# Order of the cross-attention steps: rows turned ahead of the shifted scores, tail rows both in bank 0, first maxima in slot 7

## What is computed

```python
x = x + attn_window(_layernorm(x))              # L0: 16 heads of 16, |i-j| <= 32
x = x + xattn_pad(ctx, ctx, _layernorm(x))      # keys padded per item
x = x + top2_of_8_experts(_layernorm(x))        # softmax gate, two gelu layers
x = x + attn_causal(_layernorm(x))              # L1
x = x + xattn_mask(_layernorm(x), ctx, ctx)     # one mask for all rows
x = x + quantised_ffn(_layernorm(x))            # scale is a maximum over all rows
```

## Time and profile before

| | |
|---|---|
| median of 3 runs | 2198.09 us (2197.56 to 2198.1) |
| the profiled execution: its own time, its span | 2189.82 us, 2188.2 us |
| PE busy, share of the span | 1992.9 us, 91% |
| DVE, ACT, POOL busy | 1245.5, 965.0, 688.6 us (57%, 44%, 31%) |
| granted PE clock in the mean | 0.974 |

### The profile page before, as it was taken

One profiled execution on the slowest core, in us unless ns is written; L12 is line 12 of the kernel. 1 busy time (PEld: TensorE's weight loads), 2 busy tenths in 40 slices (PEclk: granted clock), 3 DMA queues, 4 the chain that ended last, 5 costly groups with the idle time before them and its releaser, 6 DMA issues. The chain is left out here.

```text
span 2188.2 us, 51471 instructions
## 1 busy us (share of the span) xinstructions
PE 1992.9 (91%) x17362; PEld 1531.9 (70%) x17362; DVE 1245.5 (57%) x5443; ACT 965.0 (44%) x1849; POOL 688.6 (31%) x1254
## 2 busy tenths in 40 slices
PE   7999998999967999999999799999988887999869
PEld 5777776666646999999998577777666664444357
DVE  5778885566641101111115688888777775459964
ACT  3455555666632333333333255555545553357400
POOL 3566665245561000000001545553422220013400
PEclk9999999999978999999999899999999998999989
DMA  7333332233319999999995644333233321000023
GB/s 216 108 106 108 103 122 86 89 106 111 112 68 359 376 339 346 337 347 336 347 335 190 186 127 135 122 125 108 83 99 97 95 92 43 0 0 1 0 58 96
DMA packets 209108, 334.50 MB, mean 153 GB/s; under 512 B 59453, under 2 KB 193250, under 8 KB 199874
## 3 DMA queue, kind: packets, MB, share of 16 engines
q1 hardware_dynamic: 194482, 301.82, 39.6%
q0 software_dynamic: 9552, 26.10, 3.9%
q10 hardware_dynamic: 4928, 4.72, 0.6%
HBM read 193.74 MB, written 28.05 MB: 101 GB/s over the span
## 5 line engine op out<-in xcount | busy, mean ns | idle before, releaser
L1913 ACT ACTIVATE moe_h<-moe_h_ps,moe_weights 128x128 f32<-128x128 f32 x424 | 132.8, 364 | 254.3 <-PE moe_h_ps L1885 226.0
L2344 PE MATMUL ffn_prod_ps<-x_sb,ffn_weights 128*128 128x512 f32 x480 | 210.9, 599 | 9.7 <-ACT ffn_sig_q L2330 7.0
L1251 ACT ACTIVATE causal_prob<-causal_ps 128x768 f32<-128x768 f32 (+1 forms) x192 | 168.7, 879 | 113.2 <-PE causal_ps L1500 111.8
L1945 DVE TENSOR_TENSOR moe_y<-moe_y_ps,moe_weights 128x256 f32<-128x256 f32 x53 | 22.5, 425 | 328.1 <-PE moe_y_ps L1895 328.1
L1885 PE MATMUL moe_h_ps<-moe_h,moe_weights 128*128 128x128 f32 x1696 | 198.0, 275 | 0.0
L1832 POOL DMA_DIRECT2D moe_y_dram<-moe_y x71 | 39.4, 555 | 494.6 <-DVE moe_y L1945 494.6
L1885 PEld LDWEIGHTS moe_h_ps<-moe_h,moe_weights 128*128 128x128 f32 x1696 | 193.6, 192 | 0.1
L2344 PEld LDWEIGHTS ffn_prod_ps<-x_sb,ffn_weights 128*128 128x128 f32 x480 | 91.0, 192 | 127.2 <-issue 110.2
L984 DVE CUSTOM_DVE_ANT_0 causal_masked<-causal_ps,causal_causal_mask 128x256 bf16<-128x256 f32 (+1 forms) x512 | 152.4, 354 | 45.2 <-PE causal_ps L1466 43.5
L984 DVE CUSTOM_DVE_ANT_0 window_masked<-window_ps,window_window_mask 128x160 bf16<-128x160 f32 x512 | 135.3, 320 | 60.4 <-PE window_ps L1466 57.8
L1251 ACT ACTIVATE window_prob<-window_ps 128x640 f32<-128x640 f32 x128 | 90.0, 703 | 97.7 <-PE window_ps L1500 96.2
(11 more groups left out here) (376 smaller groups left out, 4675.8 us busy)
## 6 DMA issues: line engine op xcount, KB each, us to landing
moe_weights<-moe_w_in SPq DMA_DIRECT2D x53, 2180.0 KB, 9.0
q_pair<-parts SPq DMA_DIRECT2D x512, 128.0 KB
parts<-moe_w_in SPq DMA_DIRECT2D x18, 2180.0 KB, 8.9
k_pair<-parts SPq DMA_DIRECT2D x256, 128.0 KB
k_pair<-parts SPq DMA_DIRECT2D x256, 38.5 KB
moe_rows<-moe_slots_dram SPq DMA_DIRECT2D x71, 128.0 KB, 3.1
moe_y_dram<-moe_y POOLq DMA_DIRECT2D x71, 128.0 KB, 3.4
x_before_ffn_dram<-x_sb SPq DMA_DIRECT2D x16, 256.0 KB, 2.2
```

The source lines that it names most:

```text
L1251: nc.scalar.activation(out, src, ACT.Exp).then_inc(expd, 1)
L1913: nc.scalar.activation(out[:, f, :], psum[:, f // 2, (f % 2) * TM:(f % 2) * TM + TM], ACT.Gelu, bias=bias[:, f:f + 1]).then_inc(done, 1)
L2344: op = nc.tensor.matmul(prod_ps[:, slot, f, :].rearrange("p (b t) -> p b t", b=2), w[:, k, at:at + P], x_cols(n // GROUPS, k), start=(k == ...
```

## The change

Four edits, on PE, ACT and DVE; on POOL and SP no instruction moves. For steps with shifted scores of a cross item (refs 18 to 33, new helper `wide`):

1. PE turns the rows of the new item (L1598) ahead of the shifted scores of slot 0, not behind them.
2. The first half's maxima (`max_out` hf 0 and `max_rows`) go from slots 4 and 5 to slot 7: on PE ahead of the output projection, on ACT behind the exponentials of slot 6.

In tail steps:

3. Both tail halves use columns 256 on of bank 0. The second now waits for the first's evacuation (`last_ev`), and no longer for `q_lo` and `added`; ACT evacuates it in slot 4 behind the exponentials and ahead of v, where it was behind v.
4. DVE makes the low parts of q ahead of the tail's statistics in slot 2.

```diff
+        def wide(ref):
+            return active(ref, 2) and layer_at(ref, 2).pairs == 2
...
+                        if i == 2 and active(ref, 0):
+                            low_part(q_parts[par], q_ps, layer_at(ref).bq, q_hi, q_lo, t, S)
                         if i == 2 and in_tail(ref, 4):
...
-                        if i == 2 and active(ref, 0):
-                            low_part(q_parts[par], q_ps, layer_at(ref).bq, q_hi, q_lo, t, S)
...
                     act.wait_ge(last_mm, e * 2 + k + 1)
-                    if k == 1 and active(ref, 0):
-                        act.wait_ge(v_ev, t + 1)
...
-                    nc.scalar.activation(out, bank(k)[:, S:2 * S], ACT.Copy).then_inc(last_ev, 1)
+                    nc.scalar.activation(out, bank(0)[:, S:2 * S], ACT.Copy).then_inc(last_ev, 1)
...
-                        if i == 5 and in_tail(ref, 5):
-                            keep_turned(t, ref, 1)
-                        if i == 5 and active(ref, 1):
+                        if i == 5 and active(ref, 1) and not wide(ref):
                             max_rows(t, 1, 0)
...
+                        if i == 4 and in_tail(ref, 5):
+                            keep_turned(t, ref, 1)
+                        if i == 7 and active(ref, 1) and wide(ref):
+                            max_rows(t, 1, 0)
...
-                        op = nc.tensor.transpose(bank(k)[:, S + s * P:S + s * P + P],
+                        op = nc.tensor.transpose(bank(0)[:, S + s * P:S + s * P + P],
...
                         if active(ref, 1):
                             scores(t, ref, i)
+                        if i == 0 and active(ref, 0) and wide(ref):
+                            turn_normed(t, ref)
...
                         if i == 4 and in_tail(ref, 5):
-                            wait(pe, q_lo, upto(t, ref, 0))
-                            wait(pe, added, upto(t, ref, 4))
+                            pe.wait_ge(last_ev, tail_item(t, 5) * 2 + 1)
+                            if routing(ref, 6) or routing(ref, 7):
+                                pe.wait_ge(seen, tail_item(t, 6) + 1)
                             last_turn(t, ref, 1)
...
-                        if i == 4 and active(ref, 1):
+                        if i == 4 and active(ref, 1) and not wide(ref):
                             wait(pe, k_lo, self_upto(t, ref, 0))
...
-                            wait(pe, m_ev, upto(t, ref, 1, 2) - (1 if active(ref, 1) else 0))
+                            if wide(ref):
+                                wait(pe, m_ev, upto(t, ref, 2, 2))
+                            else:
+                                wait(pe, m_ev, upto(t, ref, 1, 2) - (1 if active(ref, 1) else 0))
...
                             pe.wait_ge(oT_ev, t - 2)
+                            if active(ref, 1) and wide(ref):
+                                max_out(t, 1, 0)
```

More of the change, by code:

```diff
@@ L1338, in step @@
                             keep_oT(t)
[L1339 to L1340 removed]
+                        turned_first = wide(ref) and (i == 0 and active(ref, 0) or i == 6 and active(ref, 3))
                         if active(ref, 2) and not turned_first:
```

26 lines of the change are left out of this document (11 added, 15 removed).

## The result

| | before | after |
|---|---|---|
| median of the timed runs | 2198.03 us (2197.56 to 2198.1, 4 runs) | 2180.66 us (2177.71 to 2181.0, 4 runs) |
| profiled execution, its span | 2189.82, 2188.2 | 2180.63, 2179.0 |
| PE busy, granted clock | 1992.9, 0.974 | 1997.5, 0.971 |

After / before is 0.9918 (95% interval 0.9901 to 0.9936): 17.4 us faster. The forecast was 8.6 us faster, 2189.5, with a range of 2182 to 2197. The sign was right, the size was half of the real one, and the time lies outside the range.

The account below looks back on a forecast made before the run. PE was taken as the bound, busy 91% of the span, with 1.83 us idle in a second-stage loop step. Terms 8.4 + 0.6 + 2.6 - 3.0 = 8.6 us off 2198.09 gave 2189.5, range 2182 to 2197.

Parts of the forecast that it names:

- second stage, loop, 10 steps: Loop steps of the second cross layer: each 0.84 us shorter, 8.4 in all; bounds 0.2 to 1.5 a step.
- ref 31 there: Second-stage step written out, not looped: 0.6 us gained, as L1684 starts 0.36 behind ACT there, not 0.15.
- first stage, refs 21 to 31: Eleven first-stage steps: 0.37 from ACT's chain plus 0.18 from slot 0 less 0.31, 0.24 each, 2.6 us.
- refs 18 to 20: Steps of either layer with no new work ahead to fill: gain and the 0.31 cancel, 0.
- last refs: Refs 34 to 36 of both layers: tail pairs sharing bank 0 run serially, a loss of 3.0 us (0 to 6.0).
- First maxima in slot 7: Second-stage loop step: ACT has two evacuations, not three, ahead of L1684, which comes 1.15 us earlier; step gains 0.84.
- Maxima paid again in slot 7: The two maxima transposes cost PE 0.31 us again between the evacuation of oT and the output projection.
- The second pair's 0.50: Slot 4, second stage: the 0.50 us wait ahead of the second tail transposes goes entirely; the value product starts at 1667.73.
- The DVE limit ahead of the scores: Second-stage loop: row maxima of slot 4 on DVE hold the next scores by 0.1 us, at no cost.
- Slot 0: Rows turned ahead of shifted scores: 0 in the second stage (query projection waits for DVE's add), 0.18 us in the first.
- Rival 1: The 0.42 us ahead of slot 0's query projection hangs on xT: 5.9 more gained, 2183.6; chance 0.10.
- Rivals 2, 3 and 4: 2: L1684 gain lost elsewhere, 2193.5, chance 0.17; 3: slot 7 maxima buy nothing, 2204.9, 0.07; 4: nothing seen, about 2198, 0.08.

Follow-up runs that it names:

- e1: The kernel before, run again unchanged: 2189.25 us, ratio to before 0.9996.
- e2: The changed kernel, run again unchanged: 2170.69 us, ratio to before 0.9912.
- e12: The kernel before, unchanged, once more on a further chip: 2189.15 us, ratio to before 0.9994.
- e13: The changed kernel, unchanged, once more on a further chip: 2172.02 us, ratio to before 0.9916.
- e5: The kernel before, less ACT's wait for its own value evacuation (v_ev) ahead of the second tail evacuation: 2184.32 us against 2190.1, ratio 0.9973.
- e6: The changed kernel plus a wait of ACT's value evacuation on its own tail evacuation (last_ev): 2173.44 us, ratio to before 0.9931.
- e4: The changed kernel with the first maxima back in slot 4, waiting there for the second tail evacuation: 2187.67 us, ratio to before 0.9992.
- e10: The changed kernel with DVE's low query parts behind the tail's statistics again: 2184.82 us, ratio to before 0.9946.
- e9: The changed kernel with the rows turned behind the shifted scores again: 2179.12 us against 2196.0 for before, ratio 0.9918.
- e8: The changed kernel, second tail pair in bank 1 in refs 34 to 36, DVE's output-projection add ahead of first row maxima (second stage): 2159.14 us, ratio 0.9868.
- e3: The changed kernel with the second tail pair in bank 1, evacuated behind the value with the v_ev wait: 2173.12 us, ratio to before 0.9920.

## Why the forecast was right in sign and half in size

Term by term, from the copies e1 and e2, with e12 and e13 where they differ:

| step of the prediction | forecast | measured |
|---|---|---|
| second stage, loop, 10 steps | 8.4 (0.84 each) | 11.3 (16.94 to 15.81, 1.13 each) |
| ref 31 there | 0.6 | 1.2 |
| first stage, refs 21 to 31 | 2.6 (0.24 each) | 6.7 (0.57 in each undisturbed step; 8.1 from e12, in which two steps are disturbed) |
| refs 18 to 20 | 0 | 1.4 (0.9 first, 0.5 second stage; 0.9 and 0.2 from e12 and e13) |
| last refs | -3.0 | -1.4 second stage, about -0.5 first stage from ref 34 on; its refs 32 and 33 vary too much |
| experts, up to the second stage | not in the sum | 2.1 and 2.7 |

The measured column adds up to about 21 us. The medians of the same chips differ by 18.3 in both pairs; the profiled executions of the changed kernel lie 4.3 and 1.3 below their medians. So 2 to 3 us of the column are not in the medians.

A steady step can be cut in four, at the exponentials of slot 4, at the transposes of the attention output (L1684, now L1693) and at those of the divided output (L1696, now L1705). From e1 and e2, means of the loop steps and medians of the first-stage steps from ref 23 on:

| part of the step | second stage, before and after | gain (forecast) | first stage, before and after | gain (forecast) |
|---|---|---|---|---|
| start to exponentials | 8.69, 8.69 | 0 (0) | 9.05, 8.98 | 0.07 (0.18) |
| exponentials to attention output | 3.11, 1.68 | 1.43 (1.15) | 2.61, 1.96 | 0.65 (0.37) |
| attention output to divided output | 2.04, 2.10 | -0.06 (0) | 2.11, 2.11 | 0 (0) |
| divided output to next step | 3.07, 3.32 | -0.24 (-0.31) | 3.08, 3.22 | -0.15 (-0.31) |

In both stages the second row carries 0.28 more than forecast, the largest error of a step.

**The step that failed** is the ACT chain of "First maxima in slot 7". It put the tail evacuation 0.18 behind the exponentials, "the gap that the tail has behind the value now", and L1684 1.15 earlier. Measured from the start of the slot's exponentials, L1684 came 3.16 behind them before and comes 1.71 behind now (1667.52 - 1665.81): 1.45 earlier. Of the 0.30 that the forecast lacks, 0.28 stands where the tail evacuation starts, 0.10 ahead of the end of the exponentials and not 0.18 behind it. The gap was not ACT's spacing but the wait for `v_ev`, which the diff of the change shows going out: e5 takes that wait alone out of before; the evacuation comes 0.28 earlier, and 0.21 in the first stage, and the step is shorter by as much. There the forecast likewise carried "the gap of 0.11" over: L1684 followed the exponentials by 2.62 (504.02 - 501.40), and in e2 it does by 1.97, 0.65 earlier and not 0.37. e6, with such a wait between tail and value, shows the same with a smaller size in the second stage (0.15 a step; 0.23 in the first). The wait at the very place where the forecast had its gap, between exponentials and tail, no run has.

**Maxima paid again in slot 7.** Sized 0.31, it cost 0.24 in the second stage: from the start of the divided output's transposes to the next step it is 3.32 now (1672.91 - 1669.59) and was 3.08; the two transposes take 0.29 of issue behind a wait of 0.19, and the output projection behind them issues in 1.82 and not 1.93. In the first stage it cost 0.15, half of the forecast (3.08 to 3.22), the second error there. That the exchange as a whole pays, e4 shows: 0.44 and 0.52 a step, with the wait in it that before did not have.

**The second pair's 0.50** went entirely, and the value product with it, as forecast; e10 shows it hanging on the low parts. The DVE limit ahead of the scores, forecast at 0.1, is 0.20 to 0.24 in the loop. L1693 starts 1.62 behind the value product (1.9 forecast), the loop step is 15.8 (16.1 forecast), the first-stage step 16.28 (16.6 forecast).

**Slot 0.** Right: worth 0 in the second stage (e9), with the wait in the add (e8). Rival 1 falls. In the first stage 0.07 was had of 0.18, which hides part of the other errors.

**Refs 18 to 20** were set to zero, gain and 0.31 taken to cancel. But the first stage's ref 19 got 0.45 shorter (15.16 to 14.71). There is no tail evacuation yet in these steps; ACT had the value's and the maxima's ahead of L1684 and now has the value's alone. L1693 follows the exponentials by 1.48 there and followed them by 2.01, and slot 7 costs 0.15.

**Last refs.** Right for the second stage: 1.4 lost of the forecast 1.5, if otherwise spread. The serial pair shows 1.05 + 0.63 = 1.68 of waiting in ref 34 where 1.07 stood, 0.6 and not 1.0 (about 2 was forecast), and 0.8 comes behind it in refs 35 and 36. In the first stage the loss was a third of the forecast 1.5 (0.3 and 0.8 in the two pairs). The pair, in the second stage:

```profile
1826.40 0.44 PE L1537 MATMUL causal_misc<-ident,causal_last_xn 128*128 128x128 f32 x2 [1.05 <-ACT x_sb L1313]
1827.47 0.90 PE L1693 MATMUL causal_misc<-ident,causal_o_aug 64*128 64x64 f32 x16 [0.63 <-ACT x_sb L1313]
```

**The range** had bounds of 1.5 a loop step and 0.4 in the first stage, and the loop's true value lies inside; but these ends were not carried into the time. 1.5 in ten steps alone is 6.6 more than was summed, and 2189.5 less 6.6 is 2182.9; with 0.4 in eleven steps, 2181.1, below its lower end. And the first stage's 0.57 lies outside its bound of 0.4. Rivals 2, 3 and 4 fall: of what L1684 gained, 0.06 is lost by the divided output, and the wait of the scores for DVE, now 0.20, costs no more than that; the 0.19 ahead of the maxima is in the 0.24 of slot 7.

**The experts** were not in the sum, since no instruction there was changed. They gave 2.1 and 2.7 in the profiles, and the cause is open.

## What to carry to other kernels

Before a gap between two instructions of one engine is carried into a changed order, ask what in the code makes it: a wait on the engine's own semaphore is a cost that goes with the wait. A bracket's releaser is a candidate only; an end that fits to 0.1 us (here DVE's add, not xT) is the better one, and moving that instruction into idle time can pay without any other change, here 5 us in a stage where the whole change gave 12 to 13. And where bank sharing serialises two transposes, look at what else stands between them: in the steady steps of the changed kernel the second pair doesn't wait at all, in the last refs of the second stage the sharing cost 1.5 us. When an expected time is written as an absolute number, write the difference from the kernel beside it: chips differ here by as much as the change is worth.

## What the runs showed of the hardware

- A wait of ACT on a semaphore of its own last instruction puts the second of two evacuations of about 0.38 us 0.47 to 0.57 behind the start of the first (before, e3, e6); without it that is 0.26 to 0.31, an overlap of 0.06 to 0.10. Taking it out of before gave 0.28 a step in the second stage and 0.21 in the first (e5); putting it into the changed kernel cost 0.15 and 0.23 (e6).
- The same program differs by 9 to 10 us from chip to chip, before and after alike (2198, 2196, 2190 and 2189 for before; ratios 0.9912 to 0.9918 throughout). In the four profiles of the changed kernel and its variants where before takes 2196 or more, DVE's reciprocal started 0.2 to 0.7 behind PE's transposes in some of the written-out steps of the first stage, 0.1 in all others, and its ref 31 takes 19.0 to 19.5 in place of 16.3, with ACT idle for 2.3 to 2.8.
- In each of these four profiles PE is idle for 2.2 to 2.4 us in ref 31 and the granted clock falls to 0.50 about there; in the execution shown that made the next output projection 3.62 in place of 1.89.
- Between the experts' last transposes and the second stage's first, PE was idle 13.65 in e1 and 11.77 in e2, though no instruction there was changed. DVE waited 2.76 and 0.72 for the gathered expert rows:

```profile
1208.33 1.91 DVE L1105 SCALAR_TENSOR_TENSOR x_sb<-moe_got,moe_gate,x_sb 128x256 f32<-128x256 f32 x4 [2.76 <-DMA moe_got<-moe_y_dram,moe_got_pos]
```

```profile
1197.96 1.91 DVE L1109 SCALAR_TENSOR_TENSOR x_sb<-moe_got,moe_gate,x_sb 128x256 f32<-128x256 f32 x4 [0.72 <-DMA moe_got<-moe_y_dram,moe_got_pos]
```

  All four profiles of kernels built on before (13.65 to 14.33) and all eleven built on after (11.63 to 12.19) keep to their side. The cause is open.
